# A finer count of destinations, and node jobs one step ahead of the edge job, in a four-layer graph network

## The reference

```python
edge_index = jnp.stack([src, dst])
h = jnp.maximum(_layernorm(x, axis=-1), 0.0)
x = x + _L0_gnn_ref(h, edge_index, ...)   # attention over the edges of a node, softmax by dst
h = jnp.maximum(_layernorm(x, axis=-1), 0.0)
x = x + _L1_gnn_ref(h, ...)               # two SAGE convolutions, 32 -> 64 -> 32
h = jnp.maximum(_layernorm(x, axis=-1), 0.0)
x = x + _L2_gnn_ref(h, edge_index, ...)   # neighbours both ways, a hidden layer of 128
h = jnp.maximum(_layernorm(x, axis=-1), 0.0)
x = x + _L3_gnn_ref(h, ...)               # relations with 16 bases, sum by dst
```

```python
agg = jax.ops.segment_sum(x[src], dst, num_segments=num_nodes)
deg = jax.ops.segment_sum(jnp.ones((src.shape[0],)), dst, num_segments=num_nodes)
mean = agg / jnp.maximum(deg, 1.0)[:, None]
return mean @ W_l.T + x @ W_r.T + b
```

## Time and profile before

| | us |
|---|---|
| median of 3 runs | 4597.8 |
| the profiled execution | 4597.06 |
| its span in the trace | 4595.2 |
| POOL busy in the span | 3408.0 (74%) |
| VectorE (DVE) busy | 2919.1 (64%) |
| TensorE (PE) busy | 2312.3 (50%) |
| ScalarE (ACT) busy | 951.4 (21%) |

### The profile page before, as it was taken

The page is one execution under the profiler, slowest core; times in us unless marked ns, Lnnn a source line. Parts: engine busy times, 40 slices in busy tenths (PEclk is TensorE's granted clock), DMA queues, the critical chain, the costliest instruction groups (busy, mean ns, idle before and its releaser), DMA issues. The chain is left out here.

```text
span 4595.2 us, 31284 instructions
## 1 busy us (share of the span) xinstructions
PE 2312.3 (50%) x8870; PEld 1409.5 (31%) x8870; DVE 2919.1 (64%) x3922; ACT 951.4 (21%) x1485; POOL 3408.0 (74%) x3151
## 2 busy tenths in 40 slices
PE   7820067775687740000433332067775567667763
PEld 3410044443455520000433332022222334434432
DVE  8876177775888856666311111067775799999995
ACT  0012022221455521111000000044443111111110
POOL 7777677774777747776688888777773777777776
PEclk9965555555899975555655555588887777777776
DMA  1035344442354432222122222255553111111110
GB/s 30 12 96 160 58 96 99 98 101 61 120 175 169 154 114 69 67 67 66 14 5 5 5 5 5 9 163 162 162 165 99 29 30 29 28 32 28 28 32 9
DMA packets 348973, 327.85 MB, mean 71 GB/s; under 512 B 223275, under 2 KB 295862, under 8 KB 347596
## 3 DMA queue, kind: packets, MB, share of 16 engines
q1 hardware_dynamic: 81568, 230.25, 14.0%
q0 software_dynamic: 144256, 45.62, 10.5%
q10 hardware_dynamic: 122976, 49.99, 4.7%
HBM read 170.38 MB, written 156.58 MB: 71 GB/s over the span
## 5 line engine op out<-in xcount | busy, mean ns | idle before, releaser
L547 POOL DMA_INDIRECT ring<-x_table,pos x784 | 777.7, 992 | 346.5 <-issue 243.1
L1415 POOL DMA_INDIRECT sum_table<-e_add_rows,e_add_idx x392 | 612.5, 1563 | 119.5 <-issue 118.9
L547 POOL DMA_INDIRECT ring<-con_table,pos x392 | 418.0, 1066 | 153.2 <-issue 121.6
L1967 PE MATMUL g_pX<-w,g_h_T 128*128 128x512 f32 x784 | 445.4, 720 | 157.8 <-DVEq L1821 157.8
L1785 POOL DMA_INDIRECT out_x<-g_out_rows,end_index x392 | 413.3, 1054 | 122.5 <-issue 119.2
L547 POOL DMA_INDIRECT ring<-g_table,pos x392 | 378.3, 965 | 168.9 <-issue 124.1
L547 POOL DMA_INDIRECT ring<-h_table,src x392 | 405.1, 1033 | 129.8 <-issue 123.8
L344 POOL DMA_INDIRECT x_dst<-in_x,dst x392 | 399.5, 1019 | 129.7 <-issue 129.7
L1693 PE MATMUL f_pH<-f_T,w2in 128*128 128x448 f32 x672 | 300.6, 594 | 255.6 <-DVE f_T L1581 255.6
L1467 PE MATMUL e_pS<-e_values,e_equal 128*128 128x18 f32 x784 | 167.9, 377 | 386.4 <-DVEq L1441 386.4
L165 ACT ACTIVATE norm_sq<-norm_xc 128x896 f32<-128x896 f32 x168 | 157.2, 949 | 890.6 <-DVE norm_xc L138 720.6
(11 more groups left out here) (343 smaller groups left out, 5033.2 us busy)
## 6 DMA issues: line engine op xcount, KB each, us to landing
f_sums<-sum_table ACTq DMA_DIRECT2D x126, 238.0 KB
sum_table<-c_zero SPq DMA_DIRECT2D x39, 715.0 KB
g_table<-c_g SPq DMA_DIRECT2D x42, 448.0 KB, 2.8
h_table<-a_xp SPq DMA_DIRECT2D x28, 560.0 KB, 3.5
a_x<-in_x SPq DMA_DIRECT2D x28, 448.0 KB, 5.8
b_h_node<-h_table ACTq DMA_DIRECT2D x28, 448.0 KB, 5.0
b_x_node<-in_x SPq DMA_DIRECT2D x28, 448.0 KB, 5.0
x_table<-b_x_node SPq DMA_DIRECT2D x28, 448.0 KB, 2.5
```

Source lines behind the costliest of these rows:

```text
L547: pool.indirect_dma_start(out=ring[:, t, :], out_offset=None, in_=table, in_offset=bass.IndirectOffsetOnAxis(ap=idx[:, c * C + t:c * C + t ...
L1415: pool.indirect_dma_start(out=g.sums[b], out_offset=bass.IndirectOffsetOnAxis(ap=aidx[:, c % 2, t:t + 1], axis=0), in_=add[:, c % 2, t, :] ...
L1967: last = nc.tensor.matmul(pX[d % 2][:, j * 512:(j + 1) * 512], tsb[:, 0, quad], g.w3[:, (2 * d + j) % 4, :], start=True, stop=True)
```

## The change

Stage 1: the one-hot of the low part is 256 wide (`FINE`) instead of 1024, and the factor 4 (`FOLD`) goes to the high part, 98 x 4 wide. `hot(n)` writes both for a group of 4 columns of edges. TensorE makes four matmuls of 256 columns for each column of edges instead of two of 512, each with every fourth column of the high part as stationary operand. Two matmuls of zeros open the accumulation.

The first message stage: node chunks 0 to 3 are normalized before the loop and the jobs of node chunks 0 and 1 done; round c of the loop then handles the jobs of node chunks 2c+2 and 2c+3 and of edge chunk c, and the last round has no node job. x_dst is normalized at a round's start, before VectorE waits for the gathered rows; the gathered rows are normalized after it. SP's stores and loads move with the jobs.

```diff
+FINE = 256
+FOLD = LOW // FINE
...
-        hotl = sb("hot_low", [P, 2, GROUP, LOW], f16)
-        hoth = sb("hot_high", [P, 2, C, HIGH], f16)
+        hotl = sb("hot_low", [P, 2, GROUP, FINE], f16)
+        hoth = sb("hot_high", [P, 2, GROUP, HIGH, FOLD], f16)
+        none = sb("none", [P, 512], f16)
...
-            def hot_high(c):
-                if c > 1:
-                    dve.wait_ge(hots_used, (c - 1) * (C // GROUP))
-                nc.vector.tensor_tensor(hoth[:, c % 2], bc_feat(part[:, 1, c * C:(c + 1) * C], HIGH),
-                                        bc_tile(highs, C), ALU.is_equal)
-
-            def hot_low(n):
+            def hot(n):
                 if n > 1:
                     dve.wait_ge(hots_used, n - 1)
+                nc.vector.tensor_tensor(hoth[:, n % 2].rearrange("p t h k -> p t (h k)"),
+                                        bc_feat(part[:, 1, n * GROUP:(n + 1) * GROUP], HIGH * FOLD), bc_tile(highs, GROUP),
+                                        ALU.is_equal)
                 for j in range(GROUP):
                     t = n * GROUP + j
                     last = nc.vector.tensor_scalar(hotl[:, n % 2, j, :], wide[:], part[:, 0, t:t + 1], None, ALU.is_equal)
...
-                if n % (C // GROUP) == 0:
-                    hot_high(n // (C // GROUP))
-                hot_low(n)
+                hot(n)
...
+            for half in range(2):
+                nc.tensor.matmul(pcnt[0:HIGH, half * 512:(half + 1) * 512], none[:, 0:HIGH], none[:], start=True, stop=False)
             for n in range(GROUPS):
                 pe.wait_ge(low_ready, n + 1)
                 for j in range(GROUP):
                     t = n * GROUP + j
-                    for half in range(2):
-                        last = nc.tensor.matmul(pcnt[0:HIGH, half * 512:(half + 1) * 512], hoth[:, (t // C) % 2, t % C, :],
-                                                hotl[:, n % 2, j, half * 512:(half + 1) * 512], start=(t == 0), stop=(t == ET - 1))
+                    for k in range(FOLD):
+                        last = nc.tensor.matmul(pcnt[0:HIGH, k * FINE:(k + 1) * FINE], hoth[:, n % 2, j, :, k], hotl[:, n % 2, j, :],
+                                                start=False, stop=(t == ET - 1 and k % 2 == 1))
...
+        uses = [(x, "n", k) for k in range(2) for x in ("turn", "hid0", "hid1")]
+        jobs = [("n", 0), ("n", 1)]
         for c in range(EC):
-            n, m = ("n", 2 * c), ("n", 2 * c + 1)
-            uses += [("turn", *n), ("hid0", *n), ("hid1", *n), ("turn", "hd", c), ("turn", *m), ("hid0", *m), ("hid1", *m),
-                     ("turn", "mean", c), ("hid0", "e", c), ("hid1", "e", c)]
-            jobs += [n, m, ("e", c)]
+            ahead = [("n", k) for k in (2 * c + 2, 2 * c + 3) if k < NC]
+            uses += [(x, *n) for n in ahead[0:1] for x in ("turn", "hid0", "hid1")] + [("turn", "hd", c)]
+            uses += [(x, *n) for n in ahead[1:2] for x in ("turn", "hid0", "hid1")]
+            uses += [("turn", "mean", c), ("hid0", "e", c), ("hid1", "e", c)]
+            jobs += ahead + [("e", c)]
         use, job = counted(uses), counted(jobs)
...
+            for k0 in (0, 2):
+                ns = [center_node(k) for k in (k0, k0 + 1)]
+                dve.drain()
+                for k in (k0, k0 + 1):
+                    bias(xn[:, k])
+                if k0:
+                    add_r("n", 0)
+                for n in ns:
+                    w.spread(dve, n)
+                finish_nodes(k0, ns)
+                dve.drain()
+            add_r("n", 1)
             dve.drain()
-            for k in range(2):
-                bias(xn[:, k])
-            for n in ns:
-                w.spread(dve, n)
-            finish_nodes(0, ns)
-            dve.drain()
             for c in range(EC):
                 x = g.xd[:, part(c), :]
+                more, ahead = 2 * c + 2 < NC, 2 * c + 4
+                n1 = w.center(dve, x)
+                dve.drain()
+                w.spread(dve, n1)
+                bias(x)
+                if c:
+                    add_r("e", c - 1)
+                    dve.wait_ge(filled, at(use["turn", "hd", c - 1], 1))
+                w.finish(dve, n1, hd[:]).then_inc(hd_ready, 1)
                 dve.wait_ge(rows[c % 2], GAT * (c // 2 + 1))
                 n0 = w.center(dve, ring[:, c % 2])
-                n1 = w.center(dve, x)
                 dve.drain().then_inc(ring_free, 1)
                 w.spread(dve, n0)
-                w.spread(dve, n1)
-                bias(x)
-                if c:
-                    add_r("e", c - 1)
                 w.finish(dve, n0, swap(hs))
-                if c:
-                    dve.wait_ge(filled, at(use["turn", "hd", c - 1], 1))
-                w.finish(dve, n1, hd[:]).then_inc(h_ready, 1)
...
             copy_mask(0)
-            for c in range(EC):
-                if not c:
-                    bring("n", 0)
-                    hidden("n", 0)
-                w.square(act)
-                w.square(act)
+            bring("n", 0)
+            hidden("n", 0)
+            squares()
+            keep_g("n", 0)
+            bring("n", 1)
+            hidden("n", 1)
+            roots()
+            keep_g("n", 1)
+            for c in range(EC):
+                more, ahead = 2 * c + 2 < NC, 2 * c + 4 < NC
+                squares(1)
                 if c:
                     keep_g("e", c - 1)
-                w.root(act)
-                w.root(act)
-                if c:
-                    bring("n", 2 * c)
-                    hidden("n", 2 * c)
-                keep_g("n", 2 * c)
+                roots(1)
+                if more:
+                    bring("n", 2 * c + 2)
+                    hidden("n", 2 * c + 2)
+                    keep_g("n", 2 * c + 2)
                 bring("hd", c)
-                bring("n", 2 * c + 1)
-                more = 2 * c + 2 < NC
-                if more:
-                    w.square(act)
-                    w.square(act)
-                hidden("n", 2 * c + 1)
-                if more:
-                    w.root(act)
-                    w.root(act)
-                keep_g("n", 2 * c + 1)
-                if more:
+                w.squares_then_roots(act, 1)
+                if more:
+                    bring("n", 2 * c + 3)
+                if ahead:
+                    squares()
+                if more:
+                    hidden("n", 2 * c + 3)
+                if ahead:
+                    roots()
+                if more:
+                    keep_g("n", 2 * c + 3)
+                if c + 1 < EC:
                     copy_mask(c + 1)
                 bring("mean", c)
                 hidden("e", c)
...
+            for k in range(2):
+                quads("n", k)
+                hidden("n", k)
+                product("n", k)
+            for c in range(EC):
+                more = 2 * c + 2 < NC
+                if more:
+                    quads("n", 2 * c + 2)
+                    hidden("n", 2 * c + 2)
+                    product("n", 2 * c + 2)
                 quads("hd", c)
-                quads("n", 2 * c + 1)
+                if more:
+                    quads("n", 2 * c + 3)
                 cr.turn(pe, c, run[:, :, C - 1])
-                if c + 1 == EC:
-                    cr.turn_back(pe, c)
-                hidden("n", 2 * c + 1)
-                if c + 1 < EC:
-                    cr.turn_back(pe, c)
-                product("n", 2 * c + 1)
+                if more:
+                    hidden("n", 2 * c + 3)
+                cr.turn_back(pe, c)
+                if more:
+                    product("n", 2 * c + 3)
                 quads("mean", c)
                 hidden("e", c)
                 product("e", c)
```

More of the change, by code:

```diff
@@ L245, in stage_tables @@
         wide_i = sb("wide_i", [P, LOW], i32)
-        wide = sb("wide", [P, LOW], f16)
+        wide = sb("wide", [P, FINE], f16)
         base_i = sb("base_i", [HIGH, LOW], i32)
@@ L1012, in _ @@
                 x = g.xd[:, part(c), :]
-                dve.wait_ge(rows[c % 2], GAT * (c // 2 + 1))
-                n0 = w.center(dve, ring[:, c % 2])
+                more, ahead = 2 * c + 2 < NC, 2 * c + 4
                 n1 = w.center(dve, x)
-                dve.drain().then_inc(ring_free, 1)
-                w.spread(dve, n0)
+                dve.drain()
                 w.spread(dve, n1)
```

56 lines of the change are left out of this document (34 added, 22 removed).

## The result

The changed kernel takes 4664.4 us (median of 4 runs, 4663.2 to 4668.7) against 4597.2 of the kernel before in the same session (4596.2 to 4601.0): ratio 1.0146, 95% interval 1.0129 to 1.0164. It is slower, by 67.1 us; 4687 had been forecast, 4645 to 4740 the range.

The account below looks back on a forecast made before the run. The prediction took POOL's gathers to bound the kernel before, at 36.9 us a message-stage round. It summed 4597.1 + 110 (message stage) - 20 (stage 1) = 4687 us, range 4645 to 4740.

Parts of the forecast that it names:

- The cycle behind ScalarE's order, instead of POOL's gathers, sets the round: Message stage: the gathered rows' square waits behind more ScalarE work, making rounds 45.6 us against 36.9 at POOL's pace.
- If ScalarE could pass a waiting instruction, the new order would cost nothing: Message stage: without ScalarE's strict written order, gathers would stay the bound and the time be 4570 us; chance 6%.
- A round of 45.6: Message stage cycle: 24.4 mean to end of bring, 4.9 square to scan, 16.3 scan to mean; 45.6 us.
- Scan to mean: Message stage round: the part from scan to mean, with VectorE busy throughout, keeps its 16.3 us.
- mean to the end of bring: Message stage round: from the mean until x_dst's transpose is brought, 24.4 us, averaged over nine rounds of the kernel before.
- The start, 57.3 from the stage's start to the first scan: Message stage start: node jobs and x_dst now stand ahead of the first scan, which comes at 1171.4 us before stage 1's gain.
- Last but one round 41.2, last scan 24.0 behind the mean, 8 to the mean, 18.9 to the next stage: Message stage end: last but one round 4.4 us shorter, last without node job; from last scan 27 us instead of 29.
- Stage 1, 20 us gained: Stage 1: narrower low-part compares disturb POOL's gathers less, gaining 20 us, between 0 and 31; the longer count stays covered.
- The first: Message stage: POOL's gathers stay the bound, only the end changes, 4570 us; chance 6%.
- The second: Stage 1: the count becomes too slow through weight loads or narrow compares, about 67 us longer, 4774 us; chance 6%.
- The third: Message stage: TensorE's pauses lower its clock and add 3 us a round, 4723 us; chance 15%.
- The fourth: Stage 1: its gathers gain nothing from the narrower compares, 4707 us; chance 10%.

Follow-up runs that it names:

- experiment 3: The changed kernel with ScalarE's square and root of the gathered rows moved ahead of the first node job: 4629.5 us, ratio 1.0052.
- experiment 11: The kernel of experiment 3 unchanged, run again on another chip: 4622.9 us, ratio 1.0049.
- experiment 4: The changed kernel with x_dst's and the gathered rows' normalizations interleaved again after the wait, both squares ahead of the node job: 4566.2 us, ratio 0.9919.
- experiment 1: The kernel before with only the finer count of stage 1, its message stage as before: 4571.3 us, ratio 0.9934.
- experiment 8: The kernel of experiment 1 with the low part 512 wide instead of 256 and a fold of 2: 4579.1 us in one run.
- experiment 5: The changed kernel with 20 unused TensorE transposes ahead of the carry's transpose and 20 ahead of the mean's, each round: 4656.7 us, ratio 1.0114.
- experiment 10: The kernel of experiment 3 with 40 idle transposes behind the first node chunk's transpose and 20 before the mean's, none before the carry's: 4622.0 us, ratio 1.0048.
- experiment 9: The kernel of experiment 3 with the 2 x 20 idle transposes of experiment 5 added: 4666.1 us, ratio 1.0146.

## Why the prediction was right

The sign and the mechanism held, step by step; the size was 23 us too high.

- *The cycle behind ScalarE's order, instead of POOL's gathers, sets the round.* Right: the square stands right behind x_dst's copies in the trace, POOL waits 68.4 us for room in the ring (70 to 80 forecast), VectorE 5.6 us for the square of the gathered rows in the round shown (5 forecast), and TensorE 6.09 us ahead of the carry (6 forecast); the wait of 3.0 to 4.7 us a round for x_dst's square, behind the relus, I had not named. The Trainium skill's rule (TensorE: Matmul & The Clock Gate, the section on the array's architectural detail) that ScalarE's queue is strictly first-in first-out agrees with the square at 1228.06, 4.6 us behind its data.
- *If ScalarE could pass a waiting instruction, the new order would cost nothing.* Wrong. With the square alone moved up (experiments 3 and 11) the ratio falls by 0.9 to 1.0%; with VectorE's order put back as well (experiment 4), by 2.3%. So undoing ScalarE's order alone gives back less than half. The rest comes back only with VectorE's order, which has x_dst's normalization, its wait for ScalarE included, ahead of the gathered rows: they are centered 17.5 to 19.2 us behind the mean. The working had this figure (19) as harmless, since the square came later still.
- *A round of 45.6.* It was 44.3, and eleven rounds of 1.3 are 14.4 of the 17.4 us by which the stage's forecast was too long. Scan to mean was right (16.3 forecast, 16.4), square to scan too (4.9; 4.7). The step that was mis-sized is "mean to the end of bring", 24.4: mean to scan was forecast at 29.3 and took 27.9 on average, so 23.2 or so were left for it. I had averaged nine rounds of before, and took over with them the clock that TensorE had behind the mean there. Here are the 8 us behind the mean in two rounds of before, then in two of after (start and end; busy us of PE, PEld, DVE, ACT and POOL; then the granted clock, which is 0.57 of full speed in the first row; share and GB/s of the DMA):

```profile
1257.49:1265.49 8.00, 6.82 (x14) 3.74 (x15) 7.68 (x9) 1.75 (x3) 4.80 (x6) 0.57 0.33 119
1294.43:1302.43 8.00, 6.82 (x18) 3.81 (x19) 7.68 (x9) 2.33 (x4) 5.87 (x8) 0.79 0.37 124
```

```profile
1161.33:1169.33 8.00, 6.51 (x22) 3.56 (x23) 6.93 (x8) 4.10 (x7) 5.95 (x7) 1.00 0.49 180
1204.56:1212.56 8.00, 6.62 (x18) 3.48 (x19) 6.94 (x8) 2.73 (x5) 5.87 (x8) 0.79 0.47 166
```

In the changed kernel three rounds of eleven have 1.00 there (26.9 from mean to scan) and eight 0.79 (28.1 to 28.5); before, they went to and fro between 0.57 to 0.59 and 0.79. Yet over the whole stage the clock is lower than before, 0.80 against 0.89: the low level fell on the node job behind the scan (L1167, 3.19 for 4 matmuls that take 1.77 at full level), which VectorE's work covers. That the better clock came just where the cycle hangs on it was not foreseen.
- *The start, 57.3 from the stage's start to the first scan.* 56.1. *Last but one round 41.2, last scan 24.0 behind the mean, 8 to the mean, 18.9 to the next stage.* 40.6, 23.7, 7.6, 18.0: together 2.3 us too long.
- *Stage 1, 20 us gained.* 24.5, and 27.8 in experiment 1. The narrow compare took 0.278, not 0.2, and the high part 1.774, not 1.72, so the count ended 21 us later and not 11; it was covered, as forecast. The gain was larger since the loss of the gathers fell to an eighth (29.4 to 3.7), not with the compares' time. By the Trainium skill's rule (SBUF — State Buffer, Who interferes with whom), taken as a share of busy time, 16 us had come out. Which instruction disturbs, it has right: the gathers beside narrower `tensor_scalar` compares lose less (experiments 1 and 8), while the high part's `tensor_tensor` is busy for 174 us instead of 42. That the loss goes with busy time was my reading, and the runs speak against it.
- *The rivals.* The first (gathers stay the bound if the square starts when its rows are centered, 4570) was wrong as I put it: experiment 3 does that and takes 4629, since the rows are centered late, the node job then stands behind them and the carry behind the node job. Only with the x_dst part undone too does the stage fall back on POOL's gathers (experiment 4, 4566). The second didn't come: TensorE's matmuls waited for the compares 62.4 us in all. The third, 3 us more a round by the clock, didn't come either, though one of its signs did, the lower clock over the stage; experiment 5 puts the clock's part at about 1 us. The fourth is refuted by the gathers' mean of 0.954.

The 22.9 us between forecast (+90) and result (+67.1) are thus 17.4 of the message stage, 4.5 of stage 1 and 0.9 of the attention stage, which ran that much shorter. All terms that missed by more than a microsecond missed to the same side, so nothing cancelled.

No run beat experiment 4, the finer count with node jobs ahead and x_dst where it was: 0.8% and 0.7% below before on two chips.

## What to carry to other kernels

An engine that takes work in written order makes every instruction ahead of an urgent one part of its path: before an input is prepared "early", list what then stands between the late input and its first use on each engine, the helping one too. Moving the urgent instruction up isn't enough where the work it passes feeds the same cycle, as experiment 3 shows; count the new cycle before trusting it. And where a wait for data falls away, ask what the next cycle in length is: here it took 35.4 to 37.0 us in the rounds without a wait for rows, against 36.9 for the old one, so that 44 us of removed waiting could bring little, while some 8 us of added order a round cost 98.

## What the runs showed of the hardware

- The same program had rounds at two levels of TensorE's clock: 44.2 us with the mean's seven transposes at 1.76 us, 40.9 with them at 0.98, in one execution of experiment 3; in experiment 11, the same kernel on another chip, the first twelve means were all of the second kind.
- Idle matmuls are worth what they free less what they delay: 40 of them (4.5 us) in a true pause cost nothing (experiment 10), 20 (2.35 us) ahead of the carry cost 3 us a round (experiment 9). In neither did they gain anything that the chip didn't also give without them; in experiment 5 they gained 0.7 us a round.
- Beside f16 compares of 128x1024 the gathers of stage 1 lost 27.0 us, beside 128x512 3.4, beside 128x256 0.1 to 0.2, while a compare itself takes 0.477, 0.342 and 0.278 us.
- A gather beside the scan of the message stage (L1028, 128x896 f32, 2.02 us) took 1.71 to 2.69 us instead of 0.944, in 13 rounds of the kernel before. That is all of the 18.3 us that the stage's gathers lose there.
- Weight loads of the count took 0.166 us each with every fourth column as stationary operand, against 0.124 with adjacent columns (medians); TensorE had the time.
